# Handover from each mixture of experts to its attention: another order of the last weightings, sums and norms, and filler products moved

## The reference, cut to what matters

```
x = x + tanh(g_xattn[0]) * L0_xattn(layernorm(x), ctx, ...)
x = x + tanh(g_ffn[0])   * L0_ffn(layernorm(x), ...)
x = x + tanh(g_xattn[1]) * L1_xattn(layernorm(x), ctx, ...)
x = x + tanh(g_ffn[1])   * L1_ffn(layernorm(x), ...)      # mixture of 8 experts, top 2, GELU, width 512
x = x + tanh(g_xattn[2]) * L2_xattn(layernorm(x), ctx, ctx, mask, ...)   # 16 heads, masked
x = x + tanh(g_ffn[2])   * L2_ffn(layernorm(x), ...)      # mixture of 8 experts, top 2, SiLU gate, width 256
x = x + tanh(g_xattn[3]) * L3_xattn(layernorm(x), ctx, ...)              # 16 heads
x = x + tanh(g_ffn[3])   * L3_ffn(layernorm(x), ...)
```

## Time and profile before

| | |
|---|---|
| median of 3 executions | 368.47 us (368.26 to 368.66) |
| the profiled execution's own time | 369.13 us |
| its span, first to last instruction | 367.3 us |
| mean granted TensorE clock | 0.995 |
| TensorE busy | 347.7 us (95%), 38.0 of it fillers (130) |
| VectorE busy | 278.7 us (76%) |
| ScalarE busy | 216.0 us (59%) |
| GpSimd busy | 102.9 us (28%) |

### The profile page before, as it was taken

One profiled execution on the slowest core, in us unless ns is written; L12 is line 12 of the kernel. 1 busy time (PEld: TensorE's weight loads), 2 busy tenths in 40 slices (PEclk: granted clock), 3 DMA queues, 4 the chain that ended last, 5 costly groups with the idle time before them and its releaser, 6 DMA issues. The chain is left out here.

```text
span 367.3 us, 5703 instructions
## 1 busy us (share of the span) xinstructions
PE 347.7 (95%) x2026; PEld 264.7 (72%) x2026; DVE 278.7 (76%) x640; ACT 216.0 (59%) x407; POOL 102.9 (28%) x106
## 2 busy tenths in 40 slices
PE   6999998989999999989999999999999979999895
PEld 2777584857778888864568896687878836789774
DVE  5578888489787777786777769798878869788484
ACT  1316434566988979871556674577574625566582
POOL 6211521220444617312102213023494423000230
PEclk9999998999999999999999999999999999999999
DMA  6800030000562341100001100104750000000001
GB/s 197 301 3 0 10 110 5 2 1 2 169 223 74 103 131 47 44 0 2 0 2 43 45 1 2 43 4 160 241 188 2 0 0 2 0 3 2 0 2 57
DMA packets 18676, 20.37 MB, mean 55 GB/s; under 512 B 7119, under 2 KB 10729, under 8 KB 18649
## 3 DMA queue, kind: packets, MB, share of 16 engines
q1 hardware_dynamic: 18100, 19.52, 17.0%
q0 software_dynamic: 96, 0.32, 0.4%
q10 hardware_dynamic: 453, 0.18, 0.2%
HBM read 19.26 MB, written 0.59 MB: 54 GB/s over the span
## 5 line engine op out<-in xcount | busy, mean ns | idle before, releaser
L1290 DVE TENSOR_TENSOR rlo<-banks,rhi 128x512 fp32r<-128x512 f32 x64 | 44.0, 690 | 19.7 <-ACT rhi L768 18.8
L1499 PE MATMUL banks<-hhi,wuh 128*128 128x512 f32 x128 | 51.7, 404 | 1.5 <-ACT shared L880 0.7
L774 ACT ACTIVATE banks<-banks,b1s 128x512 f32<-128x512 f32 x64 | 42.3, 661 | 16.1 <-PE banks L1501 15.8
L456 POOL TENSOR_TENSOR rstd<-var,neghalf 128x4 f32<-128x4 f32 x16 | 16.5, 1034 | 121.9 <-DVE var L964 121.9
L1501 PE MATMUL banks<-hhi,wul 128*128 128x512 f32 x128 | 50.0, 391 | 0.0
L1500 PE MATMUL banks<-hlo,wuh 128*128 128x512 f32 x128 | 49.9, 390 | 0.0
L1499 PE MATMUL banks<-rhi,wdh 128*128 128x512 f32 x96 | 39.0, 406 | 4.0 <-DVE rlo L1290 3.2
L1506 PE MATMUL banks<-heat 128*128 128x512 bf16 x130 | 38.0, 408 | 2.9 <-POOL heat L434 2.9
L860 ACT ACTIVATE shared<-banks 128x512 f32<-128x512 f32 (+1 forms) x48 | 23.5, 524 | 25.9 <-PE banks L1905 25.8
L1924 PEld LDWEIGHTS banks<-vals,shared 128*128 128x128 f32 x320 | 37.5, 192 | 0.8 <-ACT shared L860 0.6
L1924 PE MATMUL banks<-vals,shared 128*128 128x27 f32 (+1 forms) x320 | 37.5, 270 | 0.0
(11 more groups left out here) (263 smaller groups left out, 700.9 us busy)
## 6 DMA issues: line engine op xcount, KB each, us to landing
rowB<-rowd SPq DMA_DIRECT2D x32, 256.0 KB, 3.9
up_raw<-in_w SPq DMA_DIRECT2D x8, 258.0 KB, 4.3
down_raw<-in_w SPq DMA_DIRECT2D x8, 256.0 KB, 4.9
up_raw<-in_v SPq DMA_DIRECT2D x8, 256.0 KB, 2.8
down_raw<-in_v SPq DMA_DIRECT2D x8, 128.0 KB, 3.4
mats<-in_mats SPq DMA_DIRECT2D x1, 640.0 KB, 5.5
mats<-in_mats SPq DMA_DIRECT2D x1, 576.0 KB, 4.0
x<-in_x SPq DMA_DIRECT2D x2, 256.0 KB, 3.8
```

The lines of the kernel that those rows point to most:

```text
L774: nc.scalar.activation(bank[BANKS1[g % 4]][:, :], bank[BANKS1[g % 4]][:, :], ACT.Gelu, bias=b1s[p][:, c_:c_ + 1]).then_inc(q["gelu"], 1)
L1290: V.tensor_tensor(rlo[g % 4][:, :], bank[BANKS1[g % 4]][:, :], rhi[g % 4][:, :].bitcast(F32), ALU.subtract).then_inc(q["lo"], 1)
L1499: mm(o, lh, rh, start=start, stop=False)
```

## The change

At the end of mixture 1, the cast `rhi` of g = 61 goes from DVE to ACT; `normalised(8)` goes from behind the loop to behind `weigh(14)`, ahead of the last `rlo`. At the end of mixture 2, `weigh(14)` goes ahead of batch 0's update, `weigh(15)` ahead of `normalised(12)`, and POOL does its last `add` before the power for norm 12 and without waiting for `normalised(12)`. In both attentions DVE does batch 1's statistics before the first `softmax_top`, and `normalised` of batch 1 between the first two; TensorE does `transposes` of batch 1 at the start of unit 1 and not behind the scores of unit 2. Behind `queries(0)` there are fewer fillers; for n = 1 batch 1's sum is transposed before the queries. Three fillers are added before `second(1)` in the second cross attention.

```diff
-        HI_DVE1 = {g for g in range(N1 * PASSES) if g % 4 == 1}
+        HI_DVE1 = {g for g in range(N1 * PASSES - 4) if g % 4 == 1}
...
# POOL, mixture 2
                 if i < LAST:
                     split_down(i + 1, 1, C2, r)
-                else:
-                    norm(12)
-                    pool.wait_ge(ln_h, NT * 13)
                 if i == 1:
                     add(3, "r", r)
                 add(4 * i + 2, "r", r)
+                if i == LAST:
+                    norm(12)
...
# DVE, mixture 1
                 if i == LAST and n == 14:
                     weigh(0, GROUPS_ - 2, C1, "q", q)
-            normalised(8)
+                    normalised(8)
             weigh(0, GROUPS_ - 1, C1, "q", q)
             last_sum("q", q)
...
# DVE, attend
                 moe_update(n, 1)
+                statistics(base + 1)
                 softmax_top(0)
-                statistics(base + 1)
+                normalised(base + 1)
                 softmax_top(1)
-                normalised(base + 1)
...
# DVE, mixture 2
                 if g == 30:
+                    weigh(1, GROUPS_ - 2, C2, "r", r)
                     moe_update(1, 0)
                 if g == 31:
                     statistics(12)
-                    weigh(1, GROUPS_ - 2, C2, "r", r)
+            weigh(1, GROUPS_ - 1, C2, "r", r)
             normalised(12)
-            weigh(1, GROUPS_ - 1, C2, "r", r)
             last_sum("r", r)
...
# TensorE, second cross attention
             transposes(5)
+            keep_busy(bank[6], 3)
             second(1)
...
# TensorE, attend
                 transposes(base)
-                keep_busy(bank[5], 3)
-                queries(0)
-                keep_busy(bank[5], 2)
-                result_T(n, 1, bank[0], m["sum"], n + 1)
+                if n == 0:
+                    keep_busy(bank[5], 3)
+                    queries(0)
+                    keep_busy(bank[5], 1)
+                    result_T(0, 1, bank[0], m["sum"], 1)
+                else:
+                    keep_busy(bank[5], 1)
+                    result_T(1, 1, bank[0], m["sum"], 2)
+                    queries(0)
+                    keep_busy(bank[5], 2)
                 pe.wait_ge(kv["pool"], B * (n + 1))
-                keep_busy(bank[5], 2)
                 scores_of(0)
...
                     elif u == 1:
-                        if n == 1:
-                            keep_busy(bank[0], 2)
+                        transposes(base + 1)
                         transpose_of(0, 1)
...
                             scores_of(2, 0, (1,))
-                        transposes(base + 1)
```

## The result

The changed kernel takes 370.81 us (median of 20 executions, 370.2 to 373.99), the kernel before on the same chips 368.82 (20). The medians are 2.0 us apart; the ratio, which takes in the five executions of 373.0 and more, is 1.0062 [1.0045, 1.0080], or 2.3 us: slower, and above the top of my range (370.0). The profiled execution took 370.92, against 369.13.

The account below looks back on a forecast made before the run. TensorE has work 95% of the time, much of it filler, so what matters is which engine is waited for at each handover. Terms: -0.2 + 1.0 - 0.8 = 0.0, so 368.6 us against the median; range 367.5 to 370.0 (8 in 10).

Parts of the forecast that it names:

- (a): First handover: the `rhi` cast of g=61 moves from DVE to ACT; everything to `weigh(14)` comes 0.2 us earlier.
- (b): First handover: `normalised(8)` ahead of the last `rlo` makes that `rlo`, the last products and the queries 0.82 us later.
- (c): First handover: one filler less behind the queries; DVE's update moves from 171.82 to 172.42, scores only 0.17 us later.
- (d): First handover: `statistics(9)` before the first maximum holds it until 174.60, not 173.60, so +1.0 us.
- (e): Masked attention: `transposes(9)`, 0.5 us of work, moves ahead of `transpose_of(0, 1)`; nothing is won back.
- the first handover: Mixture 1 to attention 2, 162 to 187 us: value +1.0 us, ends +0.4 and +1.1.
- a rival at 0.32: The clock falls at the first handover: at most 1.65 us more on the path, 370.2 us; chance 0.32.
- (f): Second handover (293 to 316 us): `weigh(14)` before batch 0's update moves the last `rlo` and the norm 0.2 us later.
- (g): Second handover: `weigh(15)` before `normalised(12)` is hidden; mixture 2's last sum comes 1.3 us earlier.
- (h): Second handover: queries 0.2 us later, scores start at 301.75, not 302.0; `statistics(13)` is hidden before the maximum.
- (i): Second handover: the 16 fillers behind the first scores keep their 3.6 us, so the second scores come 0.25 earlier.
- (j): Last attention: `transposes(13)` replaces two fillers in unit 1, +0.05 us; its removal from TensorE's queue at 313.23 gives -0.59.

Follow-up runs that it names:

- five fillers: The changed kernel with five filler products ahead of the last three products of mixture 1: 370.32 us, ratio 1.0043.
- the norm alone: The kernel before with one edit, `normalised(8)` ahead of the last `rlo` of mixture 1: 371.26 us, ratio 1.0085.
- the wait: The changed kernel with POOL's `add_bias` waiting for both negations: 372.39 us, repeated 372.64; with `normalised(8)` also put back behind the loop, 367.96.
- the better order: The changed kernel with `normalised(8)` put back, POOL waiting for the negations, and the masked attention's old order of statistics, norm and transposes: 368.97 us, ratio 0.9988.
- the same with two fillers: The better order's kernel with two fillers behind `transposes(13)` for n = 1, in the last attention: 369.51 us, ratio 1.0003.

## Why the prediction was wrong, step by step

**Fillers before `second(1)`: -0.2.** Measured -0.21 in its column. The cause is less sure than the number: without the fillers, 17.85 was reached too where the clock did not fall. And in most timed executions of the kernel before there was no fall to cure (21 of 29 on one chip have a mean clock of at least 0.998), as I supposed in the sum; those with a fall were no slower. (By the share 0.57 that fall begins at 58.29 and lasts 3.4, not 58.36 and 3.3; nothing hangs on it.)

**(a) the cast, (b) `rlo` behind the norm, (c) the update.** `rlo` and the last products came 0.79 and 0.80 later, predicted 0.82; the update would have been 0.6 later and was 2.1. With the clock held (five fillers) the handover costs +0.99 in all, and with the norm alone +1.03.

**(d) statistics before the maximum, (e) early `transposes(9)`.** The maximum waits for statistics, as in the text. Two runs show what that is worth: with the norm's place restored and these two left as changed, 25.01; with them back too, 24.17. So (d) and (e) cost 0.84, and (a) and (c) without them give 0.88 (24.17 against 25.05 before), as my 0.2 for the cast and 0.65 for three fillers less do. With the norm's 1.03 that makes the 0.99 measured: the value was right, and its parts add up.

**The step that failed** is the value of the first handover, +1.0 with a whole clock, where +2.49 was measured. The move of `normalised(8)` made nearly all of it: 2.2 us in the medians, 1.0 by the delay and 1.5 by the clock in the profile. The clock's fall there stood as a rival at 0.32, "If it falls before 167.64, fillers, transposes and queries run at half speed": it fell at 166.87, within the wait of 1.31, and the price was 1.5 us in the profile, where I gave up to 1.65. I weighed one wait of 1.02 before without a fall more than it could bear. What I did not see is that the fall need not come where the change is: in the profiles of the five kernels with the same move the clock fell at 167 to 169 in two, at 220 to 224 in three, one of them for the second time, and at 315 in one. "Does it fall at this wait" was too narrow a question. By the mean clock 50 of the 58 executions of kernels with the moved norm have a fall, and 42 of 161 of those without it, the kernel before among them. So the move makes a fall likelier; that it does so by the wait of 1.31 is argued and not shown.

**Second handover.** (f) holds in the rows: the update starts 1.30 behind the start of the `rlo` before it (294.19 to 295.49) and not 1.12 (292.29 to 293.41), 0.2 later. The fifth column, +0.12, cannot tell it: the same code gave 107.03 and 106.44 there, and all kernels without a fall in it 106.4 to 107.5. (g) holds: the last sum came 1.5 nearer against 1.3 + 0.2. (h) holds nearly: the scores came 0.4 nearer to the update, so 0.2 net, against 0.25. (i) failed: "The 16 fillers behind the first scores keep their 3.6 us", so they did, but they were no longer what ended last. (j) was therefore never paid out in full. The last column gives -0.29, with the 0.12 ahead of it -0.17, where I had -0.8. That `statistics(13)` is "hidden here, unlike at the first handover" was right for DVE's queue and wrong for POOL's: I followed DVE behind the moved step and not POOL, whose power and `add_bias` hang on it. That is the second step that failed, a stall that the sum put at nothing. In **A rule against it** I looked at one meeting of POOL and DVE, `add(14)` with `normalised(12)`, which is absent as I said; the one that came about is another. The port's cost is shown by the wait: -0.53 and -0.54, and with it the second handover gives (0.12 - 0.84) -0.7, close to my -0.8.

**The sum.** -0.3 (start, no edit) - 0.2 + 1.0 + 1.5 (clock) - 0.2 = 1.8, which is the profile's difference. In the medians it is 2.0: there the start, with the same code, should not differ, and most executions before had no fall to lose.

**Open.** Why the clock falls at one place and not at another, and what a fall costs in the time. Inside one kernel, executions with a lone fall are by their medians 1.3 us slower than those without (five fillers), 2.2 (the better order) and 2.4 (the same with two fillers), but in the kernel before not slower at all. Two of the 20 executions of the changed kernel have a clock of 0.998 or more and took 370.39 and 370.66, hardly less than those with a lone fall (median 370.72). With five fillers and a whole clock it takes 369.9. So the 1.5 of the profile is the price in that handover, and how much of the 2.0 between the medians is the clock stays open: 0.8 by the filled kernel, next to nothing by those two executions.

## What to carry to other kernels

When a step moves earlier on one engine, follow everything that waits for it on the other engines too, down to the small operations: here statistics 4.7 us earlier, counted from batch 0's update, let a GpSimd bias addition loose on top of a 0.17 us negation that eight exponentials waited for. A short step put ahead of the last remainder of a product chain costs its whole length at the end of the chain (1.0 us here), and the clock's fall that comes with it can cost as much again and more (1.5). Compare versions by executions with the same mean clock before judging an order: the better order (366.8 without a fall) could not be told from the kernel before by its median until the clock was held.

## What the runs showed of the hardware

**Falls of the clock without idle time, and far from the edit.** In its column one fall costs 0.2 at 58, 1.5 at 167, 1.1 to 1.8 at 220 to 224, 1.6 at 315 and 3.0 at 310. At 167 it begins within a wait of 1.31, and in another profile 0.6 behind the end of one (168.6); but the same wait also passed without a fall, and TensorE shows no wait from 55.9 on before the fall at 58.3, from 215.5 on before one at 220.5 and from 304.5 on before the one at 310.7. With each retiming it turns up at 58, 167, 220, 310 or 315, or not at all. One execution of the same program has it and the next does not: 6 of 12 with the five fillers. The granted clock in all of them goes between 2.4 and 1.2 GHz (1.00 and 0.50). The Trainium skill (TensorE: Matmul & The Clock Gate, "What's actually happening") has the clock set by how busy TensorE has been recently. The direction agrees at 167, and no row bears it out at 58, 220 and 310, where TensorE had work without a wait ahead of the fall; the prediction's "the direction agrees with the drop at 58.36" rested on a wait that had ended 2.4 us earlier.

**A tiny DVE operation held for a whole POOL operation.** 128x8, 0.17 us alone, 1.24 beside a POOL addition of 1.27 that started 0.06 earlier. The Trainium skill (SBUF — State Buffer, "Who interferes with whom") says "Whoever issues first gets the shared pair for the whole instruction; the other fully blocks" of VectorE's two-port modes, and names `tensor_scalar` among the operations that can enter them. The trace agrees: POOL was first, and DVE waited 1.07 of its 1.24. Which mode the negation ran in no row shows. DVE's maximum at 309.36 beside POOL's next addition (309.27, 1.28) takes its usual 0.80.
